# Graph kernel on one core: kept lane tiles, ScalarE casts of byte rows, and one operation for 77 step constants

## The chip, the cores and the metric

The kernel runs on 1 core of one Trainium2 chip. The metric is the device time of one execution in microseconds (us). Shorter is better.

## The reference

The input is a graph of 12,500 nodes with 16 features and 400,000 edges `src -> dst`, sorted by `dst`. The reference computes two layers and a layer norm after each.

```python
edge_index = jnp.stack([src, dst])
x = _layernorm(x + _L0_gnn_ref(x, edge_index, ...), axis=-1)   # messages of a sheaf Laplacian: an MLP and two Householder mirrors for each edge
x = _layernorm(x + _L1_gnn_ref(x, edge_index, ...), axis=-1)   # two GCN convolutions
# inside _L1_gnn_ref
def gcn_conv(h, W, b):
    hw = h @ W
    msg = hw[row] * norm[:, None]
    agg = jax.ops.segment_sum(msg, col, num_segments=N)
    return agg + b
h = jnp.tanh(gcn_conv(x, W1, b1))
h = jnp.tanh(gcn_conv(h, W2, b2))
```

So values are gathered three times by `src` and summed three times by `dst`: once for the messages of the first layer and once for each convolution.

## The kernel before

The engines run five separate instruction streams and meet at semaphores. Gathers and sums are done as matrix products with 0/1 matrices ("hots"). The program goes through these stages.

**Counting and row search** (0 to 600 us). VectorE builds hots of 25 columns (`one_hots`), PE counts with them, ScalarE builds step functions. In between GpSimd (POOL) reads pieces of the sorted `dst` list in waves of 49 indirect transfers (`wave`, line 623), and `cut_rows` finds on VectorE at which edges the rows of the later sort begin. Inside `cut_rows` 77 memsets (line 1334) write the constants `s * WID` into `steps_of`, one column each. The next operation (L1336) compares them with the row lengths. At the end of `cut_rows` the indices `seg_idx` are ready, for which POOL waits to gather the 41 columns of keys. Only then VectorE goes on with `one_hots`.

**Sort and lists** (600 to 1376 us), **source rows** (1376 to 2360 us) and **messages** (2360 to 5045 us). The change doesn't touch what they compute; it only moves the clearing of `next_row` ahead in VectorE's stream.

**Collect 0** (5045 to 5700 us) sums the messages by `dst`. It runs over G2 = 293 groups of 16 tiles of 128 edges. For each group POOL gathers the rows of the group into `got` (L623); in collect 0 ScalarE also copies the keys of the group out of the gathered rows into `dst_key` (`copy_keys`, L942 to L944). VectorE makes the hots of 14 tiles in one operation (`lanes`, L1725), ScalarE those of the last 2 tiles (`far_hots2`, L923, L929, L934). VectorE multiplies the gathered rows by a 0/1 mask (L1884), PE multiplies 16 hots by the rows (L1187), and VectorE adds the product into `acc` (L1734), three groups later. Hots stand in four buffers `lane_hot2`, gathered rows in four buffers `got`. The gather of group g waits for PE to be done with group g-4.

**Two convolutions.** Each has an expand stage and a collect stage.

*Expand* (5745 to 6235 us, 6794 to 7305 us) brings the value of the source node to each edge, over G = 244 groups. SyncE's queue (SP) loads a row of 2048 node numbers into `sw_in2[q]`, q = 0 to 7, broadcast to all 128 partitions: as bf16 for even q (512 KB), as bytes for odd q (256 KB). VectorE compares it with the partition number twice (`expand_hots`, L1942), into two buffers `wide_hot2`. ScalarE reads two table addresses from memory into registers (`value_load`, L972), copies two tables (`tables2`, L973), and copies the products out of PSUM (`copy_vals`, L983, two for each group), and SP stores them to `val_rows` (L564). PE does 32 products for each group (L1221).

*Collect 1 and 2* (6235 to 6763 us, 7305 to 7808 us) are collect 0 with gathers from `val_rows` and without `copy_keys`. `dst_key` is that of collect 0, so the 14 tiles of hots that VectorE makes for group g are the same numbers in all three collects.

The lane buffers and the expand buffers are the same memory:

```python
wide_hot2 = [sb(f"wide_hotb{k}", [P, 2, 2 * CH * P], BF16, of=pf) for k in range(2)]
lane_hot2 = [wide_hot2[k % 2][:, k // 2, :].rearrange("p (t c) -> p t c", c=P) for k in range(4)]
```

## Time and profile before

| what | value |
|---|---|
| time, median of 3 runs | 7859.44 us (7837.16 to 7875.79) |
| the profiled execution's own time | 7848.39 us |
| its span | 7846.7 us |
| PE busy | 4990.0 us, 64% |
| VectorE (DVE) busy | 6626.9 us, 84% |
| ScalarE (ACT) busy | 4985.6 us, 64% |
| POOL busy | 3007.9 us, 38% |

The span is what the profile covers of the execution, from the first to the last instruction. Busy times are unions over an engine's instructions. Reading registers, branches and issuing DMAs are not counted as busy; where they hold an engine up, the profile shows idle time that ended with "issue".

### The profile page before, as it was taken

What the parts mean: (1) busy time and instruction counts of PE and PEld (TensorE: products, weight loads), DVE (VectorE), ACT (ScalarE), POOL (GpSimd) and SP (SyncE); (2) the same over time, 40 slices, a digit from 0 to 9 for tenths busy, and PEclk for the clock granted to TensorE, in tenths of its full rate; (3) what the DMA queues carried; (4) which work ended last, traced back from release to release, by engine and by line L of the source; (5) the groups of instructions that cost most, each with busy time, mean ns of one, the idle gap of its engine ahead of it and who ended that gap; (6) DMA issues with size and microseconds to landing.
All of it is one profiled execution on the core that took longest, in us unless ns stands there. A gap on an engine that the chain in (4) does not pass through costs nothing.

```text
span 7846.7 us, 258653 instructions
## 1 busy us (share of the span) xinstructions
PE 4990.0 (64%) x90754; PEld 4355.6 (56%) x90998; DVE 6626.9 (84%) x10610; ACT 4985.6 (64%) x13066; POOL 3007.9 (38%) x2219
## 2 busy tenths in 40 slices
PE   2450000667658989888888889766656656566565
PEld 1340000666557777777777777655546545456454
DVE  5789993444457999999999999888799899999998
ACT  2672130222227888888888888788846677566775
POOL 5225006666642333333333333255500177200575
PEclk9665555888886777778888777655556688766876
DMA  3000000888863333333333333233369844599443
GB/s 59 7 7 12 0 14 20 313 292 296 293 235 108 104 103 103 103 105 105 105 103 103 103 103 104 90 96 95 93 199 296 259 112 112 148 296 293 131 111 87
DMA packets 510712, 1043.85 MB, mean 133 GB/s; under 512 B 125669, under 2 KB 316485, under 8 KB 497573
## 3 DMA queue, kind: packets, MB, share of 16 engines
q1 hardware_dynamic: 376804, 761.05, 27.9%
q0 software_dynamic: 113920, 281.72, 15.0%
q10 hardware_dynamic: 19904, 0.13, 0.2%
q8 instruction: 34, 0.56, 0.0%
q14 instruction: 50, 0.40, 0.0%
HBM read 756.46 MB, written 286.18 MB: 133 GB/s over the span
## 4 chain that ended last, share of the span: by engine, by line
DVE 34%; issue 27%; PE 12%; ACT 8%; POOL 6%; DVEq 6%; DMA 3%; another core or an unknown queue 3%; ACTq 2%; POOLq 0%; SPq 0%
PE ps L1083 6%; POOL got L623 4%; DVE wide_hotb L1942 4%; PE ps L1221 3%; DVE keys L1437 3%; DVEq L1729 3%; DVE whole L1818 2%; ACT apartb L929 2%; DVE mirr L1822 2%; DVE low L1825 2%; DVE prod L1786 2%; DMA got<-val_rows,dst_idx 2%; DVE acc L1734 2%; DVE keys L1436 2%
## 5 line engine op out<-in xcount | busy, mean ns | idle before, releaser
L623 POOL DMA_INDIRECT xs_buf<-xd_rows,src_idx x488 | 877.9, 1799 | 1820.4 <-DVE mirr L1822 1678.4
L1187 PE MATMUL ps<-got,wide_hotb 128*128 128x96 bf16 x14064 | 1041.6, 246 | 656.6 <-DVE got L1884 341.8
L1187 PEld LDWEIGHTS ps<-got,wide_hotb 128*128 128x128 bf16 x14064 | 887.7, 120 | 810.4 <-issue 358.3
L623 POOL DMA_INDIRECT got<-val_rows,dst_idx x586 | 735.2, 1255 | 1376.7 <-DMA val_rows<-val_out 1079.6
L1942 DVE TENSOR_SCALAR wide_hotb<-sw_inb,slot_id 128x2048 bf16<-128x2048 bf16 x976 | 922.4, 1014 | 53.6 <-PE ps L1221 53.4
L1725 DVE TENSOR_TENSOR wide_hotb<-dst_key,iota_b 128x1792 bf16<-128x1792 bf16 x879 | 952.8, 1084 | 13.4 <-ACT dst_key L944 9.5
L1162 PEld LDWEIGHTS ps<-w2c,hid 128*128 128x128 f32 x7808 | 953.3, 199 | 14.0
L1162 PE MATMUL ps<-w2c,hid 128*128 128x32 f32 x7808 | 929.4, 279 | 20.0 <-issue 9.5
L1113 PEld LDWEIGHTS ps<-wide_tab,wide_hot 128*128 128x128 bf16 x23424 | 634.0, 102 | 527.1 <-DVE wide_hot L1719 498.7
L1221 PE MATMUL ps<-wide_tabb,wide_hotb 128*128 128x48 bf16 x15616 | 629.2, 206 | 366.6 <-DVE wide_hotb L1942 247.6
L1083 PE MATMUL ps<-row_tab,dst_hot 128*128 128x64 bf16 x15744 | 653.4, 203 | 304.7 <-issue 247.0
L1221 PEld LDWEIGHTS ps<-wide_tabb,wide_hotb 128*128 128x128 bf16 x15616 | 583.3, 111 | 412.9 <-ACT val_out L983 335.9
L1113 PE MATMUL ps<-wide_tab,wide_hot 128*128 128x32 bf16 x23424 | 659.4, 185 | 234.6 <-DVE wide_hot L1719 230.5
L1083 PEld LDWEIGHTS ps<-row_tab,dst_hot 128*128 128x128 bf16 x15744 | 574.0, 104 | 384.3 <-issue 346.5
L623 POOL DMA_INDIRECT src_key<-chunk_keys,src_idx x488 | 615.4, 1261 | 345.9 <-ACT xd_out L786 198.7
L1672 DVE COPY_PREDICATED xd_out<-row_upper,ps 128x512 f32<-128x512 uint8 (+1 forms) x384 | 217.3, 635 | 498.3 <-ACT xd_out L786 457.7
L929 ACT ACTIVATE apartb<-iota_b,rel_negb 128x128 bf16<-128x128 bf16 x1758 | 609.7, 394 | 39.8
L934 ACT ACTIVATE wide_hotb<-apartb,ones 128x256 bf16<-128x256 bf16 x879 | 446.3, 508 | 272.3 <-PE ps L1187 234.2
L786 ACT ACTIVATE xd_out<-ps 128x512 f32<-128x512 f32 (+1 forms) x384 | 202.4, 533 | 621.6 <-PE ps L1083 317.4
L1734 DVE TENSOR_TENSOR acc<-acc,ps 128x96 f32 x1367 | 342.6, 251 | 235.9 <-issue 189.1
L888 ACT ACTIVATE hid<-ps,b1c 128x1024 f32<-128x1024 f32 x488 | 516.8, 1117 | 4.1 <-PE ps L1147 4.1
L973 ACT ACTIVATE wide_tabb<-parts 128x96 bf16 x976 | 276.0, 283 | 364.2 <-issue 279.7
(413 smaller groups left out, 11022.3 us busy)
## 6 DMA issues: line engine op xcount, KB each, us to landing
dw_in<-dst_wide SPq DMA_DIRECT2D x96, 1312.0 KB
xd_rows<-xd_out SPq DMA_DIRECT2D x128, 984.0 KB
sw_in<-src_wide SPq DMA_DIRECT2D x244, 512.0 KB
sw_inb<-src_wide SPq DMA_DIRECT2D x244, 512.0 KB, 5.3
val_rows<-val_out SPq DMA_DIRECT2D x488, 192.0 KB, 4.2
sw_inb<-src_byte SPq DMA_DIRECT2D x244, 256.0 KB, 4.5
msg_rows<-msg_out SPq DMA_DIRECT2D x244, 200.0 KB, 2.5
dw_in<-dst_byte SPq DMA_DIRECT2D x32, 656.0 KB
```

Source lines behind the costliest of these rows:

```text
L623: return pool.indirect_dma_start(out=into, out_offset=None, in_=table, in_offset=bass.IndirectOffsetOnAxis(index, 0))
L888: act.activation(hid[:, :, at], ps[:, 0:4 * BANK].rearrange("p (b c) -> p b c", b=4)[:, :, at], ACT.Relu, bias=b1c[:, :]).then_inc(hid_rea ...
L929: last = act.activation(apart2[:, t, :], iota_b[:, 0:P], ACT.Abs, bias=rel_neg2[:, t:t + 1])
L934: act.activation(lane_hot2[q % 4][:, near:, :], apart2[:, 0:far, :], ACT.Relu, scale=-1.0, bias=ones[:, 0:1]).then_inc(far2_ready, 1)
L1083: last = mm(ps_unit[(3 * k + n) % 4][:, t - c, :, :], dst_hot[k % 2][:, t * P:(t + 1) * P], tab[:, part, :, :], start=part == 0, stop=part ...
L1113: last = mm(ps_x[:, h, t, :], wide_hot[s][:, half, e:e + P], wide_tab[s][:, h, at:at + 2 * D], start=half == part == 0, stop=half == 1 and ...
L1162: last = mm(ps_v[:, h * CH + t, :], hid[:, t % 4, at:at + P], w2c[:, :], start=False, stop=h == 1 and t == CH - 1)
L1187: last = mm(ps_sum[q].rearrange("p (k c) -> p k c", k=2), lane_hot2[q][:, t, :], got[q][:, :, at:at + 3 * D], start=t == 0, stop=t == 2 * ...
L1221: last = mm(ps_val[s * 2 + h][:, t, :], wide_hot2[s][:, half, e:e + P], wide_tab2[s][:, h, half * 3 * D:(half + 1) * 3 * D], start=half == ...
L1725: return v.tensor_tensor(to.rearrange("p t (j k) -> p t j k", k=2), rel.unsqueeze(2).to_broadcast(shape), iota_b[:, 0:w].rearrange("p (j k ...
L1734: v.tensor_tensor(to, to, of, ALU.add).then_inc(added, 1)
L1942: last = v.tensor_scalar(wide_hot2[q % 2][:, half, :], sw_in2[q][:, :], slot_id[:, half:half + 1], None, ALU.is_equal)
```

## The change

It has four parts.

1. Of the 14 hot tiles of each group that VectorE makes in collect 0, the first KEPT = 6 are stored to DRAM (`lane_rows`, 192 KB for each group) on SP's queue. In collects 1 and 2 they are loaded on SP's queue into the same place, and VectorE makes only the other 8. The store of group g waits for VectorE's signal of group g; VectorE waits for the store of group g-4 before it writes the buffer again; the load of group g waits for PE to be done with group g-4, and PE waits for the load.
2. In the expand stages, of the four byte rows q = 1, 3, 5, 7 two (q = 3 and 7) are turned into bf16 by one ScalarE activation of 128x2048 (`cast_row`), four groups ahead, and VectorE compares from the cast copy. ScalarE does it after the copies of every fourth group.
3. The 77 memsets become one `tensor_scalar` that multiplies `iota_f[:, 0:77]` by WID.
4. `next_row` is cleared before the sort, and SP's wait for that (`next_cleared`) goes.

The semaphores `sw_got` are renamed `moved`, and count the kept tiles' stores and loads too. The core of the diff:

```diff
+        sw_cast = [sb(f"sw_cast{k}", [P, 2 * CH * P], BF16, of=pf) for k in range(2)]
...
-            sp.wait_ge(next_cleared, 1)
...
+            def store_lanes(i, q):
+                sp.wait_ge(lhot2_ready[0], i * 4 + (q + 1))
+                sp.dma_start(lane_v[:, bass.ds(i * 4 + q, 1), :],
+                             lane_hot2[q][:, 0:KEPT, :].rearrange("p t c -> p (t c)").unsqueeze(1)).then_inc(moved[q], 16)
+
+            def load_lanes(i, q):
+                sp.dma_start(lane_hot2[q][:, 0:KEPT, :].rearrange("p t c -> p (t c)").unsqueeze(1),
+                             lane_v[:, bass.ds(i * 4 + q, 1), :]).then_inc(moved[q], 16)
+
+            def more_lanes(l):
+                with sp.Fori(1, G2 // 4) as i:
+                    for q in range(4):
+                        sp.wait_ge(pacc2_ready[l], i * 4 + (q - 3))
+                        load_lanes(i, q)
+                sp.wait_ge(pacc2_ready[l], G2 - 4)
+                load_lanes(G2 // 4, 0)
...
                 if l == 0:
                     sp.wait_ge(p3_done, 1)
+                else:
+                    sp.wait_ge(pval_ready[l - 1], 2 * G)
+                    for q in range(4):
+                        sp.wait_ge(moved[q], SW_MOVED + 16 * GROUPS_OF[q])
+                        load_lanes(0, q)
                 for q in range(8):
                     load_src(sw_in2[q], wide_got[q], q, src_byte_v if q % 2 else src_wide_v)
+                if l == 0:
+                    with sp.Fori(0, G2 // 4) as i:
+                        for q in range(4):
+                            store_lanes(i, q)
+                    store_lanes(G2 // 4, 0)
+                else:
+                    more_lanes(l)
...
+                def cast_row(i, q):
+                    loads = (G + 7 - q) // 8
+                    act.wait_ge(wide_got[q], i * 16 + ((P // 4 if q < 4 else 0) * 16 + l * 16 * loads + 16))
+                    act.activation(sw_cast[q // 4][:, :], sw_in2[q][:, :], ACT.Copy).then_inc(cast_done, 1)
...
-                with act.Fori(1, LAST) as i:
-                    for q in range(4):
-                        copy_vals(i, q)
+                with act.Fori(0, G // 8 - 1) as j:
+                    for q in range(8):
+                        copy_vals(j * 2 + (1 + q // 4), q % 4)
+                        if q % 4 == 3:
+                            cast_row(j + 1, q)
...
+                    if l > 0:
+                        pe.wait_ge(moved[q], i * 16 + (SW_MOVED + 16 * l * GROUPS_OF[q] + 16))
...
-                for s in range(SEGS):
-                    last = v.memset(steps_of[:, s:s + 1], float(s * WID))
-                step(last)
+                step(v.tensor_scalar(steps_of[:, :], iota_f[:, 0:SEGS], float(WID), None, ALU.mult))
...
+            v.memset(next_row[:, :], 0.0)
             v.memset(list_keep[:, :, :], 0.0).then_inc(list_zeroed, 1)
...
-                near = NEAR2[l]
+                near, kept = NEAR2[l], KEPT if l > 0 else 0
...
+                    if l == 0 and later(i, q, 4):
+                        dve.wait_ge(moved[q], i * 16 + SW_MOVED)
+                    lanes(lane_hot2[q % 4][:, kept:near, :], rel, near - kept, P)
...
+                    if q % 4 == 3:
+                        dve.wait_ge(cast_done, i * 2 + ((l - 1) * (G // 4) + q // 4 + 1))
+                    else:
+                        dve.wait_ge(wide_got[q], i * 16 + ((P // 4 if q < 4 else 0) * 16 + (l - 1) * 16 * loads + 16))
...
+                    row = sw_cast[q // 4] if q % 4 == 3 else sw_in2[q]
```

## Rows read from the trace of the kernel before

**Rows 1.** Windows: busy us (count) of PE, PEld, DVE, ACT, POOL; clock, DMA share, GB/s

```profile
5045.00:5700.00 655.00, 425.67 (x4720) 364.91 (x4720) 511.16 (x889) 550.52 (x2054) 325.25 (x293) 0.51 0.37 97
...
5745.00:6235.00 490.00, 315.76 (x7776) 291.70 (x7776) 463.28 (x490) 318.95 (x973) 0.00 (x0) 0.63 0.88 286
6235.00:6763.00 528.00, 304.62 (x4720) 258.24 (x4720) 488.16 (x879) 382.41 (x1177) 367.73 (x293) 0.83 0.43 116
```

**Rows 2.** Groups of instructions, 6260 to 6740 us (collect 1)

```profile
L623 POOL DMA_INDIRECT got<-val_rows,dst_idx x275 | 345.9, 1258 | 135.8 <-PE ps L1187 90.3 <-issue 44.2 <-remote 1.4
L1725 DVE TENSOR_TENSOR wide_hotb<-dst_key,iota_b 128x1792 bf16<-128x1792 bf16 x274 | 297.0, 1084 | 0.0
...
L1884 DVE TENSOR_TENSOR got<-got,dst_half 128x768 bf16<-128x768 bf16 x273 | 150.5, 551 | 1.0 <-DMA got<-val_rows,dst_idx 0.8
```

**Rows 3.** VectorE in order of time, 6500 to 6508 us (collect 1)

```profile
6502.35 1.08 DVE L1725 TENSOR_TENSOR wide_hotb<-dst_key,iota_b 128x1792 bf16<-128x1792 bf16 x1
...
6504.03 1.08 DVE L1725 TENSOR_TENSOR wide_hotb<-dst_key,iota_b 128x1792 bf16<-128x1792 bf16 x1
```

**Rows 4.** The other engines in order of time, 6504 to 6507 us (collect 1)

```profile
6505.13 0.51 ACT L934 ACTIVATE wide_hotb<-apartb,ones 128x256 bf16<-128x256 bf16 x1 [0.33 <-PE ps L1187]
...
6505.76 0.69 ACT L929 ACTIVATE apartb<-iota_b,rel_negb 128x128 bf16<-128x128 bf16 x2
```

```profile
6504.13 0.85 PE L1187 MATMUL ps<-got,wide_hotb 128*128 128x96 bf16 x16 [0.78 <-DVE acc L1734]
```

**Rows 5.** The chain of waits: a gather in collect 1, one in collect 0

```profile
6369.30 3.16 DMA got<-val_rows,dst_idx
```

```profile
5593.03 4.08 DMA got<-msg_rows,dst_idx
```

**Rows 6.** Groups of instructions, 5100 to 5680 us (collect 0)

```profile
L623 POOL DMA_INDIRECT got<-msg_rows,dst_idx x269 | 296.6, 1103 | 285.4 <-ACT dst_key L944 162.4 <-PE ps L1187 113.9 <-issue 9.1
```

**Rows 7.** Groups of instructions, 5760 to 6230 us (expand of the first convolution)

```profile
L1942 DVE TENSOR_SCALAR wide_hotb<-sw_inb,slot_id 128x2048 bf16<-128x2048 uint8 x235 | 291.5, 1282 | 25.9 <-PE ps L1221 25.9
...
L983 ACT ACTIVATE val_out<-ps 128x384 bf16<-128x384 f32 x470 | 200.9, 478 | 1.1 <-DMA val_rows<-val_out 1.0
L1942 DVE TENSOR_SCALAR wide_hotb<-sw_inb,slot_id 128x2048 bf16<-128x2048 bf16 x235 | 165.7, 747 | 0.1
L973 ACT ACTIVATE wide_tabb<-parts 128x96 bf16 x470 | 132.9, 283 | 160.4 <-issue 141.3 <-PE ps L1221 16.8
```

**Rows 8.** ScalarE in order of time, 5900 to 5909 us (expand)

```profile
5903.90 0.28 ACT L973 ACTIVATE wide_tabb<-parts 128x96 bf16 x1 [0.20 <-issue]
5904.61 0.28 ACT L973 ACTIVATE wide_tabb<-parts 128x96 bf16 x1 [0.43 <-issue]
5904.80 0.85 ACT L983 ACTIVATE val_out<-ps 128x384 bf16<-128x384 f32 x2
5905.57 0.28 ACT L973 ACTIVATE wide_tabb<-parts 128x96 bf16 x1
```

**Rows 9.** Groups of ScalarE's instructions over the whole span

```profile
L814 ACT ACTIVATE wide_tab<-parts 128x192 bf16 x488 | 153.3, 375 | 7.2 <-DMA src_byte<-turned 6.4 <-issue 0.8
...
L764 ACT ACTIVATE dst_perm<-dst_perm 128x5248 uint8<-128x5248 bf16 x1 | 4.6, 4577 | 31.2 <-DVE dst_perm L1582 31.2
...
L806 ACT ACTIVATE turned<-ps 128x1024 uint8<-128x1024 bf16 x4 | 3.8, 1074 | 0.0
```

**Rows 10.** The memset line: durations min/median/max in ns, first and last start

```profile
L1334 DVE MEMSET steps_of<- x77: 59/59/59, 51.9 to 108.1; 128x1 f32 x77
```

**Rows 11.** POOL in order of time, 100 to 125 us

```profile
102.06 0.95 POOL L623 DMA_INDIRECT found<-dst_samples,probe_i  x1 [0.30 <-issue]
122.83 0.95 POOL L623 DMA_INDIRECT keys<-key_rows,seg_idx  x1 [19.82 <-DVE seg_idx L1356]
```

**Rows 12.** VectorE's windows (clock, DMA share, GB/s last): in a wave, and without one

```profile
266.00:325.00 59.00, 8.83 (x10) 0.53 0.30 23
190.00:249.00 59.00, 58.90 (x67) 0.80 0.00 0
```

More of the change, by code:

```diff
@@ L403, in gnn_kernel @@
         rows_got = [sem(f"rows_got{k}") for k in range(4)]
-        sw_got = [sem(f"sw_got{k}") for k in range(4)]
+        moved = [sem(f"moved{k}") for k in range(4)]
         whot_ready, wtab_ready = sem("whot_ready"), sem("wtab_ready")
@@ L465, in gnn_kernel @@
         p3_done = sem("p3_done")
+        SW_MOVED = 16 * (G // 4)
+        GROUPS_OF = [(G2 + 3 - q) // 4 for q in range(4)]
+        cast_done = sem("cast_done")
         sorted_keys = keys[STEPS % 2]
@@ L583, in _ @@
                     store_vals(G // 8 - 1, q)
+            sp.wait_ge(pval_ready[1], 2 * G)
+            for q in range(4):
+                load_lanes(0, q)
+            more_lanes(2)
             sp.wait_ge(out_ready, 1)
@@ L1506, in _ @@
             other_i = other[:, :].bitcast(I32)
-            v.memset(next_row[:, :], 0.0).then_inc(next_cleared, 1)
             v.memset(rear_sum[:, 0:1], float(CPR))
@@ L1870, in turn @@
                 def turn(i, q, warm=True):
-                    rel = dst_key[:, bass.ds(i * (8 * CH) + 2 * CH * q, near), :]
+                    rel = dst_key[:, bass.ds(i * (8 * CH) + (2 * CH * q + kept), near - kept), :]
                     width = RW if l == 0 else 3 * D
@@ L1894, in collect @@
                 dve.wait_ge(acc2_added[l], G2)
+                if l == 0:
+                    for q in range(4):
+                        dve.wait_ge(moved[q], SW_MOVED + 16 * GROUPS_OF[q])
             def per_node(a):
```

22 lines of the change are left out of this document (14 added, 8 removed).

## The prediction

> **What bounds the kernel now.** I read the page first, for the shares, then the windows by stage, because the change touches five stages that have different limits. In each I looked at the groups of instructions, to see which engine has no idle time, and at the order of time, for the shortest cycle that each other engine could keep.
>
> In collect 1 VectorE is busy 488 of 528 us [rows 1]. A group costs it 1084 ns of lane hots and 551 ns of masking, with nearly no idle time before either [rows 2], and the 0.26 us of adding. One group starts 1.68 us after the other in the row quoted, and where no gap falls between them 1.64 us; over 480 us with 274 groups the mean is 1.75 us [rows 2, 3]. The 0.12 us above 1.64 are mostly the turn of the loop, once in four groups. So VectorE bounds the collects of the convolutions.
>
> In collect 0 ScalarE is busy 551 of 655 us and VectorE only 511 [rows 1]: ScalarE bounds it, with its extra copies of keys; a group takes 580 / 269 = 2.16 us [rows 6].
>
> In expand VectorE is busy 463 of 490 us [rows 1]. Its compares take 1282 ns on bytes and 747 ns on bf16, 235 of each in 470 us [rows 7]. Four groups are then 4 x 1282 + 4 x 747 = 8.12 us of VectorE, and take 4 x 470 / 235 = 8.00 us (neighbours overlap a little). VectorE bounds it, but the DMA engines are at 0.88 with 286 GB/s [rows 1], and ScalarE is close behind: from one group's first table copy to the next there are 5905.57 - 5903.90 = 1.67 us where it doesn't wait [rows 8], 6.7 us in four groups.
>
> In the row search the 77 memsets of 59 ns start from 51.9 to 108.1 us [rows 10]. That is 56 us for 5 us of work. It falls together with POOL's first wave of gathers, the last of which is at 102.06 us, and after which POOL sits idle 19.82 us for `seg_idx` [rows 11]. The second wave does the same to other work: VectorE is busy 8.8 of 59 us beside it and 58.9 of 59 us without one [rows 12]. So the engines hardly get instructions through while a wave runs; I don't know by what mechanism.
>
> **Part 1, kept lane tiles in collects 1 and 2.** Lanes shrink from 1792 to 1024 elements. From 1084 ns at 1792 and 551 ns at 768 [rows 2] the slope is 0.52 ns an element, so 1024 take 685 ns, 0.40 us less. VectorE would then need 1.64 - 0.40 = 1.24 us a group, and 1.36 with the loop's turn. What is late next:
>
> - ScalarE: from `far_hots2`'s last operation at 6505.13 to the end of the next pair at 6505.76 + 0.69 = 6506.45 [rows 4], so about 1.36 us a group with a wait between.
> - POOL: a gather takes 1258 ns and 0.30 us lie between gathers [rows 2, 11], 1.56 us. With VectorE less busy it is shorter: 1103 ns in collect 0 [rows 6], where VectorE is at 78% [rows 1], and 0.95 us beside an idle VectorE [rows 11]. That gives 1.40 and 1.25 us. VectorE will be at about 1.24 / 1.5 = 82%, so I take 1.40.
> - DMA: 0.43 x 1.75 = 0.75 us of the engines' time a group now [rows 1]. The load adds 197 KB; at expand's 286 / 0.88 = 325 GB/s that is 0.60 us. Sum 1.35 us.
> - The ring of four buffers: a gather that stands on the chain takes 3.16 us, in collect 0 up to 4.08 [rows 5]; masking 0.55, products 0.85 [rows 2, 4], some 0.2 for semaphores. (3.16 + 1.6) / 4 = 1.19 us; with 4.08 it is 1.42. The kept tiles' own ring has no POOL and no masking in it, so it is shorter.
>
> All of these stand between 1.19 and 1.56. I take 1.40 and leave the 0.12 by which the period is above its flat cycle now: 1.52 us. That is 0.23 x 293 = 67 us for each collect, 135 us for both. Ends: 1.40 us (0.35 x 586 = 205 us), which is all of VectorE's saving but the loop's turn, and 1.65 us (0.10 x 586 = 59 us), POOL unrelieved with some jitter.
>
> The SBUF page of the Trainium skill (Who interferes with whom) says that a VectorE operation on two tensors competes only with GpSimd's reads, and infers that it leaves descriptor writing alone. The rows disagree so far: gathers last 0.95, 1.10 and 1.26 us as VectorE's share rises. By that page POOL would stay at 1.56 + 0.12 = 1.68 us and the gain at 0.07 x 586 = 41 us; it is one of the rivals below.
>
> Collect 0 gets the stores: 192 KB a group, the same 0.60 us of DMA at a period of 2.16, on SP, which does nothing else there. VectorE's added wait is for a store issued four groups earlier, over 6 us before. What is queued behind that wait is lanes, masking and adding, and ScalarE has the later end. Gathers will land a little later: 0 to 15 us, I take 5. At the end VectorE waits for the last store, and at each collect's start PE for a load issued after the expand's last product instead of nothing: 1 to 3 us each, 3 in all. The loads stand on SP ahead of the next expand's first eight loads, which have a whole collect to land.
>
> **Part 2, casts.** Four groups have six bf16 compares and two on bytes: 6 x 747 + 2 x 1282 = 7.05 us of VectorE, 0.95 to 1.07 us less. The cast is 128x2048 on ScalarE. By 1074 ns at 1024 and 4577 at 5248 [rows 9] it takes 1074 + 1024 x 0.83 = 1.92 us. If it simply adds, ScalarE needs 6.7 + 1.9 = 8.6 us for four groups, more than the 8.00 of now. But 0.43 us in each 1.67 are idle time until a register is loaded [rows 8], and in the message stage, where long activations stand ahead of the same kind of table copy, 488 of these pairs have 7.2 us of idle time before them in all [rows 9]. So the queue runs ahead under a long activation. Its busy time alone is 4 x (2 x 283 + 2 x 478) = 6.1 us [rows 7] and 8.0 with the cast, less the overlap of neighbours (two copies of 0.48 end after 0.85 [rows 8]), so about 7. The DMA engines need 0.88 x 8.0 = 7.0 us. Three limits lie between 7.0 and 8.6; I take 7.5, between the register loads all hidden and one group's hidden. 0.5 x 61 = 30 us for a layer, 61 us for both. Ends: 7.1 (110 us gained), 8.6 (73 us lost).
>
> The page Advanced Engine Details and Errata of the Trainium skill (Engine Queue Depths) gives ScalarE's queue 8 entries. That would hide a whole group's registers behind a cast, and gives 7 rather than 8.6.
>
> **Part 3, memsets.** One operation takes the place of 56 us. But the wave runs until 103 us whatever VectorE does, and the 22 small operations from L1336 on will now run beside it. VectorE can be done with `seg_idx` before 103 us if each takes no more than the memsets' 1.4 us (52 + 8 + 31 = 91). Then POOL gathers keys 19.8 us earlier [rows 11], and one or two groups are counted before. Against that, counting then runs beside two bursts without a break. I take 18 us. Ends: 0 and 40 us. Part 4 moves a 60 ns operation and removes a wait on something long done: nothing, as VectorE's stream cleared `next_row` before it made the marks, for which SP waits anyway.
>
> **Sum.** 7848 - 135 - 61 - 18 + 8 = 7642 us for the profiled execution. The median of the runs is 11 us above it, so 7650 us.
>
> **The rivals.**
>
> - *The gathers bound the collects.* VectorE's 0.40 us only turns into waiting for POOL or landing rows, at 1.65 to 1.70 us. For it: POOL is the largest entry in a flat cycle now at 1.56, and the page above. Against: its duration falls with VectorE's load. Of the 135 us about 45 are left, 0.08 us for each of 586 groups, with the casts as forecast: 7650 + 135 - 45 = 7740 us.
> - *ScalarE becomes the bound of expand* at 8.6 us, the casts cost 73 us rather than give 61; collects as forecast: 7650 + 134 = 7784 us.
> - *Everything lands well*: collects at 1.40, expand at 7.1, row search 35 us: 7650 - 70 - 49 - 17 = 7514 us.
> - *The other side: kept tiles are slower to load than to make.* The DMA engines carry twice the bytes in the collects, and a gather that lands later holds up its ring. With 61 and 18 us from the other parts, slower than before takes a loss of over 71 us in 586 groups, so a period over 1.87 us, that is a ring of 7.5 us and gathers of 5.9 us where the rows have 3.16 to 4.08. At 2.0 us a group: 7859 + 146 - 71 = 7934 us. Against it: expand moves 286 GB/s, and the collects would ask for 393 KB in 1.52 us, 259 GB/s.
>
> **How the numbers follow.** The forecast, with both collects at 1.45 to 1.6, 0.55. Gathers bound 0.19. ScalarE bound 0.10, everything well 0.09, the other side 0.07. 7650 us. The range takes in the gathers' rival and most of the ScalarE one, and ends above the best case: 7550 to 7800 us. This kernel's measurement can tell about 0.5%, 39 us: slower 0.07, the last case; within it 0.05, where the gathers bind and ScalarE does too (7740 + 134 = 7874 us); faster than 7820 us the other 0.88.
>
> **What would show it.** In the windows, collects 1 and 2 at about 450 us (410 to 485), expand at 460 to 480, collect 0 at 655 to 670, counting over at about 580 us instead of 600. Lanes at 0.68 us x 586 and a cast of 1.9 us x 122. ScalarE's idle time before table copies should shrink behind casts. POOL's gathers should fall from 1258 ns to about 1100 in the collects; if they don't, the first rival holds. If PE waits for loads of the lane tiles rather than for VectorE or gathers, the last one does. The DMA share of the collects should be 0.85 to 0.9. The prediction is wrong if a transfer's landing takes over 5 us in the collects, or if PE in expand waits for ScalarE most of the time.

## The result and the profile after

| | median | range |
|---|---|---|
| before | 7859.12 us | 7798.25 to 7884.14, 10 runs |
| after | 7901.43 us | 7882.65 to 7916.06, 10 runs |

The ratio is 1.0053 (95% interval 1.0037 to 1.0070): slower by 0.5%, where 2.7% faster was forecast. The profiled execution took 7895.04 us, with a span of 7893.3 us against 7846.7 us. Where the 46.6 us are (counting is over when VectorE reads the last counts, the source rows when ScalarE's last copy of them starts; a collect reaches from the first to the last start of ScalarE's hots, an expand from the first to the last start of its copies out of PSUM; the last column is the change):

| stage | before | after | difference |
|---|---|---|---|
| counting over, at | 601.3 | 615.3 | +14 |
| source rows over, at | 2323 | 2321 | -2 |
| collect 0 starts, at | 5062.7 | 5055.4 | -7 |
| collect 0 | 632.4 | 660.8 | +28 |
| expand 1, 2 | 486.3, 486.9 | 493.7, 493.7 | +7, +7 |
| collect 1, 2 | 517.7, 514.2 | 520.0, 520.4 | +2, +6 |

So it isn't one loss. Neither of the two large gains came, and collect 0, which only got the stores, lost the most. (Expand 2 of the kernel before ends at 7285 us, not at 7305.) The windows by stage, as [rows 1], collect 0 first, then expand and collect of each convolution:

```profile
5040.00:5720.00 680.00, 425.10 (x4720) 364.50 (x4720) 515.28 (x882) 556.09 (x2051) 324.10 (x293) 0.51 0.62 178
5769.00:6264.00 495.00, 321.95 (x7776) 296.98 (x7776) 398.60 (x485) 402.12 (x1033) 0.00 (x0) 0.60 0.88 283
6264.00:6790.00 526.00, 327.69 (x4660) 285.69 (x4661) 394.46 (x874) 380.99 (x1174) 309.42 (x293) 0.76 0.80 226
6830.00:7325.00 495.00, 317.38 (x7776) 293.40 (x7776) 397.85 (x484) 400.93 (x1034) 0.00 (x0) 0.61 0.88 283
7325.00:7850.00 525.00, 337.01 (x4656) 294.05 (x4656) 393.85 (x873) 379.45 (x1172) 311.06 (x293) 0.73 0.78 220
```

VectorE did get its work taken away: 463 to 399 us in expand, 488 to 394 us in collect 1. The stages didn't get shorter. In the collects the DMA share went from 0.43 to 0.80 and PE's granted clock from 0.83 to 0.76 (1.0 is 2.4 GHz, 0.5 is 1.2 GHz). The groups of instructions in collect 1 (6290 to 6770 us), against [rows 2]:

```profile
L663 POOL DMA_INDIRECT got<-val_rows,dst_idx x273 | 288.4, 1056 | 191.0 <-PE ps L1241 169.6 <-issue 18.9 <-remote 2.5
...
L1777 DVE TENSOR_TENSOR wide_hotb<-dst_key,iota_b 128x1024 bf16<-128x1024 bf16 x272 | 187.0, 687 | 0.0
L1938 DVE TENSOR_TENSOR got<-got,dst_half 128x768 bf16<-128x768 bf16 x273 | 151.6, 555 | 33.1 <-DMA got<-val_rows,dst_idx 25.5 <-issue 5.9
```

Lanes take 687 ns (685 forecast), and the gather's own time on POOL fell from 1258 to 1056 ns. But POOL's idle time grew from 136 to 191 us, nearly all of it for PE, which means for a free `got` buffer, and before masking (L1938) there are now 25.5 us of waiting for gathered rows, where there was 0.8. The chain of waits in collect 1, by share, first of the kernel before (6260 to 6740 us), then after with two of its longest pieces, against the 3.16 us of [rows 5]:

```profile
by line: POOL got L623 30.5%; issue 21.7%; DVEq L1867 12.6%; DVE wide_hotb L1725 8.0%; DMA got<-val_rows,dst_idx 7.0%; DVE got L1884 5.9%; DVE acc L1734 5.1%; PE ps L1187 3.8%; DVEq L1725 1.5%; DVEq L1734 1.2%; DVEq L1888 0.8%; DVEq L1883 0
```

```profile
by line: DMA got<-val_rows,dst_idx 21.7%; PE ps L1241 21.5%; issue 20.2%; DVEq L1919 13.2%; DVE wide_hotb L1777 7.4%; DVE got L1938 6.9%; DVE acc L1786 3.1%; DVEq L1786 1.4%; ACT wide_hotb L974 1.4%; DVEq L1938 1.2%; DVEq L1942 0.8%; POOL g
...
6700.71 5.57 DMA got<-val_rows,dst_idx
...
6726.29 6.06 DMA got<-val_rows,dst_idx
```

A landing gather went from 7.0 to 21.7% and is now the largest entry; PE's products went from 3.8 to 21.5%. Before, the largest entry was POOL's own time on its gathers (30.5%), and VectorE's lanes had only 8.0%; all of VectorE's entries together, with its register loads (DVEq), come to 36%. So POOL stood about level with VectorE in the kernel before already. In collect 0 (5100 to 5680 us) two pieces of the chain, and POOL's group, are

```profile
5607.05 5.04 DMA got<-msg_rows,dst_idx
5621.66 5.04 DMA got<-msg_rows,dst_idx
```

```profile
L663 POOL DMA_INDIRECT got<-msg_rows,dst_idx x258 | 282.5, 1095 | 299.4 <-PE ps L1241 241.8 <-ACT dst_key L984 50.6 <-issue 7.0
```

with 5.0 us where [rows 5] has 4.08, and POOL waiting 242 us for PE where [rows 6] has 114. The groups in expand (5790 to 6240 us), against [rows 7]:

```profile
L1023 ACT ACTIVATE val_out<-ps 128x384 bf16<-128x384 f32 x440 | 194.7, 485 | 0.0
L2003 DVE TENSOR_SCALAR wide_hotb<-sw_inb,slot_id 128x2048 bf16<-128x2048 bf16 x220 | 155.5, 749 | 47.2 <-PE ps L1275 46.6
L2003 DVE TENSOR_SCALAR wide_hotb<-sw_inb,slot_id 128x2048 bf16<-128x2048 uint8 x110 | 136.4, 1282 | 1.2 <-PE ps L1275 1.1
L1013 ACT ACTIVATE wide_tabb<-parts 128x96 bf16 x440 | 114.7, 285 | 86.1 <-issue 58.4 <-PE ps L1275 25.8
L1028 ACT ACTIVATE sw_cast<-sw_inb 128x2048 bf16<-128x2048 uint8 x55 | 104.5, 1901 | 0.0
L2003 DVE TENSOR_SCALAR wide_hotb<-sw_cast,slot_id 128x2048 bf16<-128x2048 bf16 x110 | 77.9, 750 | 39.5 <-ACT sw_cast L1028 38.9 <-PE ps L1275 0.6
```

The cast takes 1901 ns (1.92 us forecast), and its compare 750 instead of 1282 ns. 55 casts in 450 us are 8.18 us for four groups, against 8.00. PE and VectorE now wait for ScalarE (waits and chain of the same window):

```profile
PE ps L1275 <- ACT wide_tabb L1013: 131.1, 121, 1.9
...
DVE wide_hotb L2003 <- ACT sw_cast L1028: 38.9, 53, 1.2
```

```profile
by line: ACTq L1012 42.3%; issue 24.0%; ACT val_out L1023 11.3%; ACT wide_tabb L1013 8.0%; PE ps L1275 4.6%; ACTq L1013 3.7%; ACT sw_cast L1028 1.6%; DMA val_rows<-val_out 1.2%; ACTq L1018 1.2%; ACTq L1022 0.7%; ACTq L1036 0.6%; DVE wide_ho
```

L1012 is the `value_load` of a table's address: 42% of the chain. In the row search VectorE has `seg_idx` ready at 65 us instead of 122, and then gets little done: in the window from 100 to 200 us it is busy 59.80 us before and 32.99 after. In order of time:

```profile
64.83 0.19 DVE L1408 CAST seg_idx<-seg_f 128x41 int32<-128x41 f32 x1
...
82.92 0.17 DVE L1346 TENSOR_SCALAR step_at<-src_lohi 128x7 f32 x1 [12.21 <-remote]
...
148.03 0.17 DVE L1346 TENSOR_SCALAR step_at<-src_lohi 128x7 f32 x1 [62.24 <-issue]
...
169.86 0.17 DVE L1346 TENSOR_SCALAR step_at<-src_lohi 128x7 f32 x1 [18.99 <-remote]
```

### The profile page after: what moved, and what is told of

Read it like the earlier page. It is cut to its first block, busy times and chain, and to the rows that moved or that the text cites. A ratio compares the mean times of both kernels' runs of the same rounds, so it can differ in the third digit from the quotient of the medians.

```text
span 7893.3 us, 263457 instructions
## 1 busy us (share of the span) xinstructions
PE 5086.1 (64%) x90998; PEld 4424.4 (56%) x90998; DVE 6323.0 (80%) x10534; ACT 5158.5 (65%) x13188; POOL 2885.8 (37%) x2219
## 4 chain that ended last, share of the span: by engine, by line
DVE 29%; issue 28%; PE 11%; ACT 9%; DVEq 6%; ACTq 6%; DMA 6%; POOL 3%; another core or an unknown queue 1%; SPq 0%; POOLq 0%
PE ps L1135 7%; ACTq L1012 5%; DMA got<-val_rows,dst_idx 3%; DVE keys L1490 3%; PE ps L1241 3%; DVEq L1781 3%; DMA got<-msg_rows,dst_idx 2%; DVE whole L1870 2%; DVE mirr L1874 2%; DVEq L1919 2%; DVE low L1877 2%; DVE prod L1838 2%; DVE keys L1489 2%; DVE acc L1786 2%; ACT val_out L1023 2%
## 5 line engine op out<-in xcount | busy, mean ns | idle before, releaser
L1241 PE MATMUL ps<-got,wide_hotb 128*128 128x96 bf16 x14064 | 1093.8, 255 | 642.3 <-DVE got L1938 396.4
L1241 PEld LDWEIGHTS ps<-got,wide_hotb 128*128 128x128 bf16 x14064 | 947.6, 126 | 788.3 <-issue 594.0
L663 POOL DMA_INDIRECT got<-val_rows,dst_idx x586 | 620.5, 1059 | 1515.4 <-DMA val_rows<-val_out 1095.2
L1777 DVE TENSOR_TENSOR wide_hotb<-dst_key,iota_b 128x1024 bf16<-128x1024 bf16 (+1 forms) x879 | 720.7, 820 | 14.8 <-ACT dst_key L984 9.1
L2003 DVE TENSOR_SCALAR wide_hotb<-sw_inb,slot_id 128x2048 bf16<-128x2048 bf16 x732 | 631.0, 927 | 102.9 <-PE ps L1275 101.5
L969 ACT ACTIVATE apartb<-iota_b,rel_negb 128x128 bf16<-128x128 bf16 x1758 | 609.5, 394 | 40.0 <-ACT rel_negb L963 0.3
L1938 DVE TENSOR_TENSOR got<-got,dst_half 128x768 bf16<-128x768 bf16 x879 | 487.1, 554 | 93.2 <-DMA got<-val_rows,dst_idx 75.8
```

What stands on the lines that cost most here:

```text
L663: return pool.indirect_dma_start(out=into, out_offset=None, in_=table, in_offset=bass.IndirectOffsetOnAxis(index, 0))
L969: last = act.activation(apart2[:, t, :], iota_b[:, 0:P], ACT.Abs, bias=rel_neg2[:, t:t + 1])
L1241: last = mm(ps_sum[q].rearrange("p (k c) -> p k c", k=2), lane_hot2[q][:, t, :], got[q][:, :, at:at + 3 * D], start=t == 0, stop=t == 2 * ...
L1777: return v.tensor_tensor(to.rearrange("p t (j k) -> p t j k", k=2), rel.unsqueeze(2).to_broadcast(shape), iota_b[:, 0:w].rearrange("p (j k ...
L1938: v.tensor_tensor(upper_row, whole_row, half, ALU.mult).then_inc(lhot2_ready[l], 1)
L2003: last = v.tensor_scalar(wide_hot2[q % 2][:, half, :], row[:, :], slot_id[:, half:half + 1], None, ALU.is_equal)
```

## The experiments

They fall into two sets with different levels of time: the kernel before takes 7843 to 7863 us in the first and 7522 to 7526 us in the second. The expectations call them the first and the second chip. That the level belongs to a chip isn't shown: the record numbers the chips of the second set 1, 12 and 11, those of the first 4 and 11, so number 11 stands in both. Every ratio compares with runs of the kernel before taken beside it, and stages are in us, as above. The stages come from one trace for each kernel.

**Each part alone (second set).** `e1_lanes_only` is part 1 with the small part 4; `e2_casts_only` part 2 with part 4; `e3_constants_only` part 3; `e6_one_cast` is e2 with only q = 7 cast:

```diff
-                    if q % 4 == 3:
+                    if q == 7:
...
-                    row = sw_cast[q // 4] if q % 4 == 3 else sw_in2[q]
+                    row = sw_cast[1] if q == 7 else sw_in2[q]
```

> Only the kept lane tiles, no casts, memsets as before. The transfers' theory (the kept tiles' bytes make every gather land later, and the ring of four buffers takes over from VectorE) says collect 0 is about 28 us longer than before and collects 1 and 2 are 2 to 6 us longer each, the whole about 35 us slower (7895). If instead the combination with the casts or the shifted start were at fault (the rival), collects 1 and 2 alone would be shorter by tens of us and the time below 7859.

> Only the casts (and the clearing of next_row moved). If ScalarE is the bound of expand with them, each expand takes 492 to 495 us against 486, and the whole is about 15 us slower (7874). If the casts lose only because of what the lane tiles leave on SP's queue or on the DMA engines (rival), expand drops to 460 us and the whole to about 7800.

> Only the one operation in place of 77 memsets. The burst theory (while POOL's waves of gathers run the other engines get few instructions through, and the early count is only moved into the burst) says that seg_idx is ready at 65 us instead of 122 us and the keys' gathers start 20 us earlier, and that counting still ends no earlier than before: at 600 to 620 us. The rival: counting ends 20 us earlier, at 581 us, and the 14 us of loss seen with all parts come from something else.

> Casts only, and of the four byte rows only q = 7 is cast, every eight groups. ScalarE's theory: eight groups need 8 x 1.67 + 1.9 = 15.3 us of ScalarE and 10 x 0.747 + 6 x 1.282 = 15.2 us of VectorE, against 16.0 us before, so about 15.6: each expand 12 us shorter (474 us), the whole about 7835. If the DMA engines at 0.88 bind (rival), expand stays at 484 to 486 us and the whole at 7859.

| kernel | ratio | collect 0, 1, 2 | expand 1, 2 | counting over |
|---|---|---|---|---|
| e7_before_again | - | 632.6, 504.0, 510.9 | 487.7, 488.2 | 417.1 |
| e1_lanes_only | 1.0000 (0.9981 to 1.0018) | 658.7, 514.6, 507.3 | 486.6, 487.5 | 417.5 |
| e2_casts_only | 1.0024 (1.0005 to 1.0043) | 632.9, 508.1, 525.0 | 495.2, 495.7 | 417.4 |
| e3_constants_only | 0.9979 (0.9953 to 1.0005) | 634.0, 504.1, 508.1 | 487.7, 487.0 | 416.2 |
| e6_one_cast | 0.9978 (0.9955 to 1.0002) | 632.4, 504.2, 524.2 | 482.2, 486.0 | 418.9 |
| e8_after_again | 1.0046 (1.0029 to 1.0063) | 661.9, 515.2, 508.2 | 495.5, 493.8 | 416.4 |

Each stage's loss goes with its own part: collect 0 is 26 to 29 us longer wherever lanes are stored, expand 6 to 8 us wherever two rows in eight are cast. So e2 came out as expected. For e1 the stages say +33 us against e7, but the ratio keeps the whole within 14 us of no change, where 35 us slower was expected: that expectation was missed. The two differ because e7 is one execution with short collects. In kernels that leave them alone collects 1 and 2 together take 1012 to 1033 us in this set, with lanes stored and loaded 1022 and 1023 (e1, e8); so only collect 0's loss is clear in e1. One cast in eight groups (e6) costs nothing and gives an expand 2 to 6 us, where 12 were expected. e3 could not show much here: in e7 the 77 memsets take 1.7 us together (52.2 to 53.9 us), not 56, and `seg_idx` is ready at 66 us with them and at 65 without.

**Does the whole repeat, and does the level of time go with the set or with the kernel?**

> The kernel before, unchanged, for a trace from the chip of the next three kernels. The two chips seen so far differ: spans 7846.7 us on the first, and 7504 to 7536 us for four nearly equal kernels on the second, almost all of it in counting (601 against 417 us) and in the source rows' stage (942 against 707 us). Theory C (the head's stalls and the slower row stage belong to a chip, not to a kernel): this trace shows either both of them (seg_idx at about 122 us, counting over at about 600) or neither (66 and 417). Rival: one without the other. In the collects of layers 1 and 2: a period of 1.70 to 1.75 us.

> The whole change again. Sum of its parts as measured alone (lanes 5 us slower, casts 22 us slower, constants 20 us faster, each against the kernel before on the second chip, each with some 15 us of uncertainty): +7 us, ratio 1.001. Theory C: on a chip without the stalls beside gather waves the ratio is 1.000 to 1.003; on one with them the constants' operation costs 14 us rather than nothing and the ratio is 1.004 to 1.006 as in the first result. Rival (the parts disturb each other): above 1.006 on either.

It does: 7557.31 us, ratio 1.0046. The 1.000 to 1.003 forecast from the sum of the ratios was too low, though the uncertainties of the four ratios together nearly cover the gap; the stages' own differences (29 + 8 + 11 + 6 - 3 = 51 us of the spans' 57) are those of the parts. The stalls beside gathers go with the set and not with the kernel: here counting is over at 416 to 417 us in both kernels, and in the first set at 586 to 632.

**Lanes and loads apart (second set).** `e4_no_loads` is e1 without `load_lanes`, `more_lanes` and PE's wait for them, so that collects 1 and 2 use whatever lies there for 6 of 14 tiles, and the output isn't the reference's. `e5_spare_loads` loads as e1 does, but into a buffer that nobody reads, and VectorE makes all 14:

```diff
+        spare = [sb(f"spare{k}", [P, KEPT * P], BF16, of=pf) for k in range(4)]
...
-                sp.dma_start(lane_hot2[q][:, 0:KEPT, :].rearrange("p t c -> p (t c)").unsqueeze(1),
+                sp.dma_start(spare[q][:, :].unsqueeze(1),
...
-                near, kept = NEAR2[l], KEPT if l > 0 else 0
+                near, kept = NEAR2[l], 0
```

> Part 1 alone, with the stores of collect 0, but without any load in collects 1 and 2: VectorE makes 8 tiles a group, the products of those collects take whatever lies in the other 6 tiles, so agg isn't the reference's. Theory A (the loads' transfers delay the gathers and thereby the ring of four buffers): with them gone, landings are back at 3.4 us, the period of collects 1 and 2 falls from about 1.72 to 1.45 us, each is some 70 us shorter, the time 130 us below the kernel before, ratio 0.983. Theory B (ring, POOL and the engines' hand-overs bind at about 1.7 us even without the loads; VectorE's 0.40 us had no worth): period stays at 1.65 to 1.72, ratio 0.995 to 1.0. Collect 0, which has the stores in this kernel too: some 25 us longer than in the kernel before by both, 658 against 633 us.

> The same loads as in part 1, but into a buffer that nothing reads, and VectorE makes all 14 tiles in each collect, as before: the result is the reference's. Theory A: VectorE's 0.40 us come back on top of the longer landings; both limits stand close together, so the period of collects 1 and 2 goes to 1.80 to 1.95 us, each 25 to 60 us longer, ratio with collect 0's 25 us 1.010 to 1.020. Theory B: the transfers are hidden, collects 1 and 2 as before, ratio 1.003 (collect 0 alone).

Measured: e4 7384.24 us, ratio 0.9821 (0.9804 to 0.9837); e5 7615.95 us, ratio 1.0125 (1.0108 to 1.0142). With e7 and e8 they make a square (us a group in collect 1, the mean distance from one group's first product to the next; in brackets the mean time from a gather's start on POOL to its last landing signal):

| | VectorE makes 14 | VectorE makes 8 |
|---|---|---|
| no loads | 1.71 (3.45), e7 | 1.50 (3.31), e4 |
| loads | 1.88 (4.15), e5 | 1.75 (4.06), e8 |

The windows of the four in collect 1, in the order e7, e4, e5, e8:

```profile
5920.00:6400.00 480.00, 266.02 (x4494) 224.49 (x4492) 464.40 (x843) 363.83 (x1124) 339.28 (x282) 0.91 0.43 115
```

```profile
5940.00:6355.00 415.00, 239.27 (x4456) 201.61 (x4453) 365.43 (x835) 360.69 (x1115) 285.57 (x279) 0.99 0.52 132
```

```profile
5945.00:6475.00 530.00, 337.34 (x4501) 288.39 (x4501) 476.86 (x844) 364.42 (x1126) 338.75 (x282) 0.71 0.75 210
```

```profile
5960.00:6450.00 490.00, 316.46 (x4478) 276.28 (x4476) 377.10 (x839) 363.32 (x1123) 294.41 (x282) 0.75 0.79 226
```

Down a column, the loads cost 0.17 us a group beside 14 tiles and 0.25 beside 8. Along a row, six tiles less are worth 0.21 us without loads and 0.13 with them, of 0.40 us of work. Collect 2 repeats it: 1.75, 1.49, 1.89 and 1.74 us in the order e7, e4, e5, e8. Theory A is what the two ratios say; B is out. That the lanes' saving and the loads' cost cancel (1.71 to 1.75) is the whole result of part 1 in collects 1 and 2. Landing gathers make up 8.8 and 10.8% of the chain in e7 and e4, and 26.1 and 37.9% in e5 and e8. The load of the kept tiles itself is never what PE waits for: in e8 it has landed at least 0.5 us before PE starts on its group, in every group of collect 1 behind the first eight. The stores' cost in collect 0 is there in both, 658.2 and 656.7 us.

**Half the bytes (first set).** `e9_kept3` is e1 with `KEPT = 3`.

> Part 1 alone with 3 kept tiles a group instead of 6: half the bytes stored and loaded, VectorE makes 11 tiles (1408 elements, about 0.20 us less than for 14). Theory A (what a load costs goes with its bytes; the loads alone cost 0.17 us a group, and all of VectorE's 0.40 us are worth 0.24): half of each, 1.72 - 0.12 + 0.09 = 1.69 us in collects 1 and 2, 10 us less in each; collect 0 645 us, 12 longer; ratio 0.998 to 1.001. Rival (the cost goes with the number of transfers, not with their bytes): 1.75 to 1.8 us, collect 0 +25 us, ratio 1.005 or more.

7830.95 us, ratio 0.9993 (0.9966 to 1.0019); collects 637.4, 511.4 and 511.4 us, that is +5, -6 and -3 against the kernel before (+12, -10 and -10 expected). The rival, that the cost goes with the number of transfers (+25 us in collect 0), is out. Half the bytes cost collect 0 well under half of the 28 us. The -6 and -3 say nothing by themselves: in kernels that leave them alone collects 1 and 2 take from 500 to 530 us in this set.

**What moves the collects that nobody changed.** VectorE's work for a group is the same in all of them, but POOL's own time on a gather isn't, and the length goes with it. The two collects of e18 (a kernel of the row search below, with collects as before) lie near the two ends, 6245 to 6715 and 7275 to 7775 us:

```profile
L623 POOL DMA_INDIRECT got<-val_rows,dst_idx x278 | 316.6, 1139 | 153.6 <-PE ps L1188 135.9 <-issue 17.7
```

```profile
L623 POOL DMA_INDIRECT got<-val_rows,dst_idx x277 | 397.7, 1436 | 105.5 <-issue 73.2 <-PE ps L1188 32.3
```

VectorE's lanes take 1087 and 1085 ns there, the collects 500.2 and 529.8 us (1.70 and 1.82 us a group), and in the second POOL's gathers are 57% of the chain. Over all 22 such collects of both sets the gather's mean lies between 1136 and 1436 ns, and the period follows it (correlation 0.95). With 0.30 us between gathers, POOL alone needs 1.44 to 1.74 us a group. What sets the gather's time isn't known.

**PE's clock.** In e8 PE's group of 16 products takes 1.16 us on average and in e4 0.86, at clocks of 0.75 and 0.99. Together with the 0.75 us of landing that is about the difference of four periods, 4 x 0.25 us, so the clock could have been part of the cost. `e15_fill_lanes` is e1 with spare products, `e14_fill_before` the kernel before with the same:

```diff
                     last.then_inc(pacc2_ready[l], 1)
+                    for _ in range(8 if l > 0 else 0):
+                        mm(ps[:, 0:P], ident_b[:, :], ident_b[:, :], start=True, stop=True)
```

> Part 1 alone with the same spare products. Theory A1 (of the 0.26 us a group that the loads cost against the kernel without them, 0.19 come from later landings, 0.07 from PE's slower clock, since each enters the ring of four by a fourth): period 1.75 goes to about 1.67 us, 20 us less a collect than with part 1 alone, ratio 0.995 to 0.997. Theory A2 (the slow clock is the main cost): period 1.50 to 1.58, 45 to 70 us less a collect, ratio 0.983 to 0.989. Theory A3 (PE's clock is a consequence of its waiting and has no part in the cost): period stays at 1.72 to 1.76, ratio 1.000 to 1.003.

> The kernel before with eight spare 128x128x128 products behind each group of collects 1 and 2, into a part of PSUM that nothing reads. They should lift PE's granted clock from 0.83 to 0.91 to about 1.0 there. VectorE bounds these collects at 1.64 us flat, so by the prediction's reading little changes: period 1.70 to 1.76 us, ratio 0.997 to 1.001. Rival (PE's slow groups of 1.46 us make part of the 0.1 us above the flat cycle): period 1.65 to 1.68, 15 to 25 us less a collect, ratio 0.994 to 0.996.

e15 7893.10 us, ratio 1.0037 (1.0019 to 1.0055); e14 7871.93 us, ratio 1.0017 (0.9998 to 1.0036). The windows of collect 1, e15 first:

```profile
6280.00:6760.00 480.00, 354.56 (x6560) 312.52 (x6557) 368.42 (x818) 354.15 (x1094) 293.24 (x275) 0.99 0.79 224
```

```profile
6260.00:6740.00 480.00, 352.98 (x6480) 310.13 (x6480) 452.33 (x809) 348.76 (x1077) 337.14 (x270) 0.99 0.42 114
```

The clock is at 0.99 and the group at 0.86 us in both, and the period stays at 1.76 (after: 1.76) and 1.77 (before: 1.76). So the slow clock isn't the main cost: A2, 45 to 70 us less a collect, is out. Between A1 (0.07 us a group from the clock) and A3 (none) this doesn't decide, as the spare products (L1231) stand on the chain themselves:

```profile
by line: issue 21.5%; PE ps L1227 18.7%; DMA got<-val_rows,dst_idx 17.6%; DVEq L1909 14.8%; DVE wide_hotb L1767 7.8%; DVE got L1928 6.7%; PE ps L1231 4.5%; DVE acc L1776 3.3%; DVEq L1776 1.6%; DVEq L1928 1.2%; DVEq L1932 0.8%; ACT wide_hotb
```

4.5% of 480 us are 0.08 us a group, as much as A1 would give back.

**ScalarE in expand (first set).** `e12_early_registers` is e2 with the registers loaded ahead of the wait; `e13_early_alone` is the kernel before with that alone; `e16_fill_expand` is e12 with eight spare products of 128 columns behind each group.

```diff
+                        if h == 1 and ahead:
+                            ats = tables_at(i, q + 2)
                         act.wait_ge(pval_ready[l], i * 8 + (2 * q + h + 1))
                         if h == 1 and ahead:
-                            tables2(i, q + 2)
+                            tables2(i, q + 2, ats)
```

> Part 2 alone, but ScalarE loads the two registers of the next tables before it waits for PE's product, not after. Theory A (in expand with the casts ScalarE is the bound, since each group waits for PE, then 0.6 us for registers, then copies): four groups take 7.2 to 7.7 us instead of 8.1, expand 440 to 470 us instead of 495, ratio 0.990 to 0.996. Rival (DMA at 0.88 to 0.90 with 288 GB/s or the ring of eight byte rows binds expand whatever the engines do): expand stays at 485 to 495 us, ratio 1.001 to 1.003.

> The kernel before with nothing but the early register loads of the run above. If VectorE bounds expand without the casts (8.0 us for four groups), this changes nothing: expand 487 us, ratio 0.999 to 1.001. If it is shorter by over 10 us an expand, ScalarE's order held VectorE up in the kernel before too, and step one of the prediction was wrong on expand.

> The casts with early register loads, and eight spare products of 128 columns behind each group of expand. If PE's clock (0.6 to 0.7) is part of expand's cycle now that each table copy waits for a product, PE's groups shorten, and expand goes from 480 to 450 to 465 us, ratio 0.992 to 0.996. If DMA (0.92, 296 GB/s) or ScalarE's busy time of 365 of 450 us binds, expand stays at 475 to 482, ratio 0.998 to 1.000. If the spare products stand in PE's way, it is over 485.

| kernel | ratio | expand 1, 2 |
|---|---|---|
| e12_early_registers | 0.9991 (0.9967 to 1.0015) | 481.1, 477.6 |
| e13_early_alone | 1.0002 (0.9984 to 1.0019) | 486.0, 486.0 |
| e16_fill_expand | 0.9985 (0.9964 to 1.0007) | 477.8, 479.8 |

The order of the register loads takes nothing off a kernel that VectorE bounds (e13), and 13 to 18 us off each expand once ScalarE bounds it (e12 against 494 to 496). Both of e12's forecasts missed: 440 to 470 us was too hopeful, and the rival's 485 too high. In e12 and e16 (windows of expand 1)

```profile
5760.00:6210.00 450.00, 284.61 (x7211) 262.05 (x7207) 370.62 (x452) 364.68 (x959) 0.00 (x0) 0.68 0.92 296
```

```profile
5780.00:6230.00 450.00, 322.94 (x9120) 294.66 (x9119) 373.01 (x455) 366.56 (x966) 0.00 (x0) 0.97 0.93 298
```

```profile
PE ps L1239 <- ACT wide_tabb L977: 112.6, 104, 1.9
ACT wide_tabb L977 <- PE ps L1239: 85.0, 115, 1.3
```

A faster clock with spare products gains nothing (0.68 and 0.97, the same length); the spare products are 3.0% of e16's chain, 13 us, so a gain of that size would be hidden. What keeps four groups at 7.96 us in e12 (450 us for 56.5 of them) is either the circle that the waits show, PE for tables and tables for PE's product, with register loads still 27% of the chain, or the DMA engines at 0.92. I made no run that tells these two apart.

**The row search.** `e11_constants_again` is e3 once more, now in the first set; `e18_keys_held` adds one wait:

```diff
             pool.wait_ge(keys_stored, 16)
+            pool.wait_ge(hot_free, 4)
             for c in range(COLS):
```

> Part 3 alone a second time, for its trace if the chip is one with stalls beside gather waves: there VectorE should show one gap of about 60 us between 85 and 150 us, and counting should be over at about 615 us instead of 601, as with the whole change. On a chip without the stalls: counting over at 416 us, as the first time.

> The constants in one operation, and the key gathers held back until four groups are counted. On the first chip: if the unbroken burst of gathers stalls VectorE, its longest gap between 60 and 160 us is under 35 us instead of 62, and counting is over at 590 to 603 us instead of 613; if not, the gap stays at 60 us or the end at 613. On the second chip: counting over at 416 us, nothing told.

VectorE's longest gap from e11, and those from e18, in order of time:

```profile
148.25 0.20 DVE L1292 TENSOR_SCALAR step_at<-src_lohi 128x7 f32 x1 [62.28 <-issue]
```

```profile
113.11 0.17 DVE L1293 TENSOR_SCALAR step_at<-src_lohi 128x7 f32 x1 [28.02 <-remote]
...
172.16 0.17 DVE L1293 TENSOR_SCALAR step_at<-src_lohi 128x7 f32 x1 [33.58 <-remote]
```

The part alone repeats the stall (62.3 us here, 62.24 in the whole change), and a pause between the two bursts breaks it up. The end is less clear: counting is over at 613.0 us in e11 and at 609.5 in e18 (590 to 603 expected). And six more traces of this set whose row search isn't changed, e9, e12, e13, e14, e15 and e16, have it at 585.8, 605.8, 609.5, 631.5, 622.6 and 629.0. Against that scatter the 14 us of the first comparison say nothing. Next to the three that were measured beside it (e14, e15, e16) e18 is 13 to 22 us earlier, while e11 is 3 to 27 us later than those beside it (e9, e12, e13); one trace each can't settle it. Single executions took 7878.79 us (e11) and 7835.33 us (e18), both within the range of the kernel before.

**A kernel faster than both (second set).** `e19_best` is e12 with the constants in one operation and the held key gathers, without any lane stores or loads.

> Casts with early register loads, constants in one operation with key gathers held until four groups are counted, no lane tiles stored or loaded. Expands 478 to 481 us instead of 487, 15 us for both; the row search between 0 and 20 us shorter on a chip with the stalls, 0 to 10 on one without; collects as in the kernel before. 15 to 35 us of 7500 or 7860: ratio 0.9955 to 0.998. If the small gains don't stand together, 0.999 to 1.001.

7498.60 us, ratio 0.9972 (0.9957 to 0.9986), as expected. Expands 482.0 and 482.8 us, a little over the 478 to 481 expected, counting over at 415.0, collect 0 633.3. Against e7 the expands give 11 us and counting 2, of the 24 us by which the medians differ; the rest isn't placed.

## Why the prediction was wrong

**The collects: the step that failed is "All of these stand between 1.19 and 1.56. I take 1.40".** The parts were right one by one: lanes at 0.69 us, POOL's gather down to 1.06 us, DMA at 0.80 of its time. What failed is that the limits were set side by side and the largest taken, which put the loads' effect on the gathers at nothing. Without any load, e4 has 1.50 us (the forecast's 1.40 plus 0.12 is 1.52, so that step held); with the loads it is 1.75. The term that was missing is that of the loads themselves. I charged them with 0.60 us of DMA time, which fits under 1.40, and took a gather's landing as at most 4.08 us, which left the ring at 1.42. Measured, landings grew by 0.6 to 0.75 us on average in the second set (by about 0.4 in the first, whose traces lack many landing signals), pieces of up to 6.7 us stand on the first set's chain, and a group lost 0.25 us. I had written that a landing of over 5 us would make the prediction wrong. As a sign that was too coarse, since single gathers land that late without any load too: in collect 1 it is 4 of 289 in e7 and 36 of 289 in e8. That the loads are the cause is shown by e4 and e5; that it acts through late gathers is read from the traces of the second set. In the first set the chain's share alone would not show it, as e18's collect 1 has 21.3% of landing gathers without any load. My picture is that VectorE takes the gathers in order and each late one adds to the period while the other limits are near; no run tests it. Why 0.75 us of mean landing costs 0.25 us of period, and not the 0.19 that the ring of four makes of it, isn't settled; PE's clock may be the rest of it, which e15 can't tell.

The reading of the kernel before was off as well. "VectorE bounds the collects", with 0.12 us over its flat cycle "mostly the turn of the loop", leaves out POOL, whose gathers were 30.5% of the chain and whose time moves the period between 1.70 and 1.82 us. So the 1.75 us that the gain was counted from is itself one draw from that range. And VectorE's idle time holds a register load too: in `add_group` it stands behind the wait for PE, as ScalarE's does in expand, and is 23% of e4's chain (13% before). Moving it ahead of the wait wasn't tried.

PE didn't wait for the lane loads themselves (e8), so the rival "slower to load than to make" was right in its place, contention in the collects, but not in the point from which it decides: it asked for over 1.87 us, since it counted on gains in the other parts that weren't there.

**Collect 0: "0 to 15 us, I take 5" measured 28.** The stores bring the DMA share from 0.37 to 0.62 and gathers on the chain from 4.1 to 5.0 us. That ScalarE bounds this stage doesn't cover it, as its keys come out of the gathered rows themselves.

**Expand: "Three limits lie between 7.0 and 8.6; I take 7.5" measured 8.18.** The second rival was right in its mechanism. The queue does run ahead under the cast, but only for what stands ahead of the next wait: in order of time after a cast two groups go without idle time, and the third waits for PE and then for its registers.

```profile
5901.39 0.47 ACT L1013 ACTIVATE wide_tabb<-parts 128x96 bf16 x2
...
5903.64 0.28 ACT L1013 ACTIVATE wide_tabb<-parts 128x96 bf16 x1 [1.01 <-PE ps L1275]
5904.69 0.28 ACT L1013 ACTIVATE wide_tabb<-parts 128x96 bf16 x1 [0.78 <-issue]
...
5906.93 1.90 ACT L1028 ACTIVATE sw_cast<-sw_inb 128x2048 bf16<-128x2048 uint8 x1
```

The message stage that I took as evidence [rows 9] doesn't have that wait between activation and register load: that was the step that failed here. The queue of 8 entries in the page Advanced Engine Details and Errata (Engine Queue Depths) of the Trainium skill doesn't contradict this: a deep queue didn't help here, where the load stands behind a wait, and moving it ahead of the wait (e12) gave 13 to 18 us.

**The memsets: 18 us, measured nothing that can be told.** `seg_idx` came 58 us earlier, and the key gathers started 16 us earlier (106.9 instead of 122.8), against 19.8 forecast. VectorE's own work beside the now unbroken burst came later, which the step had named and not priced.

**The gathers' own time.** They fell to 1.06 us, below the 1.10 assumed, so the rival of unrelieved gathers is out. The page SBUF — State Buffer (Who interferes with whom) of the Trainium skill infers that such VectorE operations leave the descriptor writing alone, by which their time would have stayed; the fall doesn't bear that out, though no run shows what sets their time. The reason that I gave was off too. I had tied them to VectorE's busy share. In the square they are 1206 and 1205 ns beside 14 tiles (e7, e5), with VectorE busy 97% and 90%, and 1025 and 1050 ns beside 8 (e4, e8), at 88% and 77%. POOL's group in e5 and in e4:

```profile
L662 POOL DMA_INDIRECT got<-val_rows,dst_idx x282 | 339.9, 1205 | 191.3 <-PE ps L1228 147.6 <-issue 43.7
```

```profile
L652 POOL DMA_INDIRECT got<-val_rows,dst_idx x279 | 286.0, 1025 | 130.2 <-PE ps L1216 126.5 <-issue 3.7
```

Between 90% and 88% lie 180 ns, so it isn't the share. Nor is it the number of tiles alone, as [rows 6] have 1103 ns beside 14, and the two collects of e18 have 1139 and 1436; what decides stays open.

The sum by terms (first result, spans): collects 1 and 2 -135 forecast, +8 measured; collect 0 +5, +28; expands -61, +14; head -18, -2 at the end of the source rows, and -6 in the messages, which the change doesn't touch; transitions +3, +3.

## What to carry to other kernels

Work that is taken off the bounding engine and put on DMA queues isn't free when the same stage waits for gathers in a shallow ring: price a transfer by what it does to the landings of those already there; here it cost 0.17 to 0.25 us a group at a DMA share of 0.8. Where three or four limits stand within 20% of each other, look at the chain of waits before calling one of them the bound, and expect a period above the largest of them; a run with the work simply left out (e4) shows at once what the best case is worth. Before a few us in one stage are read as an effect, see how far that stage moves in kernels that leave it alone (here 30 us). Before giving an engine more work, look at what stands between its wait and its next useful instruction: a register load ahead of the wait rather than behind it gave back twice what the casts had cost.

## What the runs showed of the hardware that was not expected

- The same kernel runs at two levels, 7859 and 7522 us, and the record has both under one chip number (11), so whether the level belongs to the chip is open. The difference lies in two stages: counting with its gather waves (over at 586 to 632 against 415 to 419 us) and the source rows (942 us long against 708). Collects and expands differ by less than 3%.
- In the first set the other engines nearly stop beside bursts of small indirect gathers: VectorE is busy 1.72 of 64 us in e11, and PE 4.93. In the same window of e7 (second set), with POOL as busy, they are busy 63.74 and 42.53 us.

```profile
85.00:149.00 64.00, 4.93 (x25) 2.38 (x25) 1.72 (x3) 1.00 (x4) 48.46 (x52) 0.50 0.25 42
```

- A register load from SBUF takes ScalarE 0.28 us (median of 976) in the trace; over 0.5 us are 73 of them before and 106 with the casts.
- The same indirect gather takes POOL 1136 to 1436 ns on average in collects with the same work on all engines.
- With 8 spare products a group PE's granted clock read 0.97 to 0.99, where it was 0.68 to 0.84 without, and no stage got shorter by it.
